# Corrected guesses for the row sums of the first attention, and down products interleaved with gate and up in the first feed forward

## The reference, cut to what matters

```
def _L0_xattn_ref(q, k, v, gamma):          # 8 heads over D = 256, 32 rows each
    qk = jnp.einsum('bhdq,bhdl->bhql', qh, kh) * scale
    sm = jax.nn.softmax(qk, axis=-1)
    ret = jnp.einsum('bhql,bhdl->bhdq', sm, vh)
    return gamma * ret.reshape(B, Dv, Lq)

def _L0_ffn_ref(x, gate_up_packed, gate_up_scales, down_packed, down_scales):
    w_gu = _dequant_fp4(gate_up_packed, gate_up_scales, 128)    # 2816 x 512
    w_down = _dequant_fp4(down_packed, down_scales, 128)        # 512 x 1408
    gate, up = split(jnp.einsum('bsh,oh->bso', x, w_gu))
    y = jnp.einsum('bsi,hi->bsh', jax.nn.silu(gate) * up, w_down)
    return y / jnp.sqrt(jnp.mean(y * y, axis=-1, keepdims=True) + 1e-6)

x = x + _L0_xattn_ref(_layernorm(x), ctx_2048, ctx_2048, gamma)
x = x + _L0_ffn_ref(_layernorm(x), ...)
x = x + _L1_xattn_ref(_layernorm(x), ctx_2048, ...)
x = x + _L1_ffn_ref(_layernorm(x), ...)
```

## Time and profile before

| | us |
|---|---|
| median of three runs | 2041.46 |
| profiled execution | 2041.32 |
| its span | 2039.7 |
| PE busy | 1789.8 (88% of the span) |
| DVE busy | 1562.4 (77%) |
| ACT busy | 1234.9 (61%) |
| POOL busy | 886.1 (43%) |
| dn_scale, 1408 KB, from issue at 402.8 to landing | 13.6 |
| raw_dn, 2816 KB, from issue at 402.3 to landing | 10.7 |

### The profile page before, as it was taken

How to read it: one execution, slowest core, us unless ns; L and a number is a source line. 1 busy time by engine, 2 the same in 40 slices (tenths; PEclk the granted TensorE clock), 3 DMA queues, 4 the chain that set the end, 5 groups by cost and what they waited for, 6 DMA issues and landing times. The chain is left out here.

```text
span 2039.7 us, 32890 instructions
## 1 busy us (share of the span) xinstructions
PE 1789.8 (88%) x11326; PEld 795.2 (39%) x11326; DVE 1562.4 (77%) x2892; ACT 1234.9 (61%) x2016; POOL 886.1 (43%) x908
## 2 busy tenths in 40 slices
PE   3997897688999987984989999999999988579998
PEld 0322222233344433542534444444444444234443
DVE  5899998582836627876899999999999965784433
ACT  4886776361644612441469999999999983322111
POOL 5565565160623510002038888888887880000000
PEclk9999999898999998996989999999999998789999
DMA  9764560010000002100025565555555544000000
GB/s 197 203 156 93 128 146 19 28 59 0 1 0 0 0 0 83 36 15 26 0 52 108 106 109 107 109 105 110 110 108 106 110 99 191 6 1 21 21 21 21
DMA packets 318045, 143.31 MB, mean 70 GB/s; under 512 B 273872, under 2 KB 290256, under 8 KB 316752
## 3 DMA queue, kind: packets, MB, share of 16 engines
q1 hardware_dynamic: 317904, 141.50, 31.1%
HBM read 70.15 MB, written 4.19 MB: 36 GB/s over the span
## 5 line engine op out<-in xcount | busy, mean ns | idle before, releaser
L1471 ACT ACTIVATE a_prob<-a_psS,a_bias,q_scale 128x1024 uint8<-128x1024 f32 x512 | 610.8, 1209 | 25.5 <-PE a_psS L1364 24.0
L1400 DVE TENSOR_REDUCE a_tops<-a_psM 128x1 f32<-128x512 f32 x1024 | 622.4, 675 | 1.8 <-PE a_psM L1354 0.3
L1450 POOL CAST a_wide<-a_pairs 128x2048 int16<-128x2048 uint8 x256 | 481.8, 1894 | 95.8 <-DMA a_pairs<-a_prob 87.5
L1354 PE MATMUL a_psM<-KT,QO 128*128 128x512 bf16 x1024 | 372.3, 387 | 5.9 <-PEq L1148 2.2
L1364 PE MATMUL a_psS<-KT,QO 128*128 128x512 bf16 x1024 | 305.2, 380 | 3.0 <-ACT a_prob L1471 3.0
L1376 PEld LDWEIGHTS a_psO<-V,a_wide 128*128 128x128 f16 x4096 | 175.2, 96 | 144.1 <-DVE QO L1413 23.0
L761 POOL TENSOR_TENSOR g_sum<-g_sum 128x512 f32<-128x512 f32 x88 | 126.8, 1441 | 197.6 <-DVE g_sum L826 197.6
L458 ACT ACTIVATE prob<-psT 128x512 f32<-128x512 f32 x256 | 145.5, 613 | 101.6 <-PE psT L637 101.0
L1376 PE MATMUL a_psO<-V,a_wide 128*128 128x32 bf16 x4096 | 181.3, 177 | 20.4 <-DVE QO L1413 15.6
L935 PE MATMUL g_psY<-raw_dn,g_hT 128*128 128x512 f32 x352 | 162.4, 622 | 26.3 <-DVE raw_dn L786 15.8
L514 DVE TENSOR_REDUCE rmax<-psS 128x1 f32<-128x512 f32 x256 | 161.4, 668 | 25.2 <-PE psS L623 25.2
(11 more groups left out here) (203 smaller groups left out, 2881.4 us busy)
## 6 DMA issues: line engine op xcount, KB each, us to landing
xs<-in_x SPq DMA_DIRECT2D x64, 256.0 KB, 7.9
cs<-in_ctx SPq DMA_DIRECT2D x64, 256.0 KB, 9.6
KT<-in_w SPq DMA_DIRECT2D x2, 4096.0 KB, 21.8
raw_gu<-in_gu SPq DMA_DIRECT2D x4, 1408.0 KB, 8.1
vs<-in_ctxT SPq DMA_DIRECT2D x16, 256.0 KB, 3.2
k_cT<-in_ctxT SPq DMA_DIRECT2D x16, 256.0 KB, 2.8
a_pairs<-a_prob SPq DMA_TRANSPOSE x256, 2.7
out<-x_sb SPq DMA_DIRECT2D x16, 256.0 KB, 2.0
```

What stands on the lines that cost most here:

```text
L1354: pe.matmul(psM[n % NM][:, :], QOf[:, i * P:(i + 1) * P], KTf[:, keys:keys + 512], start=True, stop=True).then_inc(shown, 1)
L1400: v.reduce_max(tops[i // JOIN % NB][:, i % JOIN, c:c + 1], psM[n % NM][:, :], AX.X).then_inc(topped, 1)
L1450: pool.tensor_copy(wide[i % NV][:, :, :, :].rearrange("p k c q -> p k (c q)"), both).then_inc(widened, 1)
L1471: act.activation(prob[i % NP][:, k * HK:(k + 1) * HK], psS[g % NS][:, :], ACT.Exp, scale=q_scale[:, i:i + 1], bias=bias[i // JOIN % NB][:, ...
```

## The change

In `mix_rows` the four reciprocals are gone. ACT now takes the logarithm of the sums and then the exponential of its negative (`logs`, `rinv`, both 128 x 512), which gives a guess of 1/s; DVE corrects the guess r to r (2 - s r) with two instructions at places 8 and 10, the second of them multiplied into `weighed`. The four parts of `collect` stand at the places 0, 1, 2 and 4.

The rows of the feed forward's first chunk are prepared inside `mix_rows`: in the last step DVE normalises them (`first_rows`), ACT makes the high part at places 10 to 13, POOL the low part, and SP transposes both with a DMA each. The normaliser of all 16 tiles moves into the feed forward, behind group 1 of chunk 0.

In `gated_ffn` the down products of group m - 3 stand between the two sides of group m and behind the second. At the fourth group of a chunk none stand, and two groups' worth at the fifth. The four tiles of rows have a bank `psY` each. The down weights come in three DMAs and are unpacked one group after the other: DVE moves and masks the bits, ACT gives the value, POOL multiplies with the scale. Later chunks are normalised, split and transposed by DMAs at groups 5 to 8 of the chunk before, so PE has no transposes left. The loop over the middle chunks is written out. Some semaphores are shared between blocks.

```
-    INVERT, STATS = (5, 7, 9, 11), (1, 3)
+    COLLECT, INVERT, STATS = (0, 1, 2, 4), (8, 10), (1, 3)
...
+                if i == 1:
+                    act.activation(e_sums[b][:, :], psE[:, :], ACT.Copy).then_inc(o_read, 1)
+                if i == 2:
+                    if j:
+                        act.wait_ge(rinv_ready, j)
+                    act.activation(logs[:, :], psE[:, :], ACT.Ln).then_inc(o_read, 1)
+                if i == 3:
+                    act.wait_ge(o_read, 3 * (j + 1))
+                    act.activation(rinv[b][:, :], logs[:, :], ACT.Exp, scale=-1.0).then_inc(rinv_ready, 1)
...
-                v.reciprocal(rinv[:, at], e_sums[j % 2][:, at]).then_inc(inverted, 1)
+                if i == 0:
+                    v.wait_ge(rinv_ready, j + 1)
+                    v.scalar_tensor_tensor(out=e_sums[b][:, :], in0=e_sums[b][:, :], scalar=-1.0, in1=rinv[b][:, :],
+                                           op0=ALU.mult, op1=ALU.mult).then_inc(corrected, 1)
+                if i == 1:
+                    v.wait_ge(corrected, j + 1)
+                    v.scalar_tensor_tensor(out=weighed[b][:, :], in0=e_sums[b][:, :], scalar=2.0,
+                                           in1=weighed[b][:, :], op0=ALU.add, op1=ALU.mult).then_inc(inverted, 1)
...
+            def first_rows():
+                own = Counter(v, env["norm_own"])
+                v.wait_ge(scales_in, 16)
+                own.count(v.tensor_copy(env["gu_scale"][:, :, :], gu_half[:, :, :]))
...
+                for k in range(TPC):
+                    v.tensor_scalar(xn[:, k, :], x_sb[:, k, :], env["mv"][:, k, 0:1], rstd[:, k:k + 1],
+                                    ALU.subtract, ALU.mult).then_inc(first_xn, 1)
...
+            def take_y(t, k):
+                v.wait_ge(squared, TPC * t + k + 1)
...
+                v.tensor_copy(y[t % 2][:, k, :], psY[k][:, :]).then_inc(y_taken, 1)
...
+                    for i in SIDES:
+                        fold(m, i)
+                        if t and p == TAKE:
+                            take_y(t - 1, 2 * i)
+                            take_y(t - 1, 2 * i + 1)
+                    if m:
+                        hidden(m - 1)
+                    if t == 0:
+                        unpack_down(p)
+                        if p == 1:
+                            normaliser(v, env)
+                    if t and p == ROOTS:
+                        finish_roots(t - 1)
...
+            def due(m):
+                groups = [m - LAG] if m >= LAG else []
+                if m % FG == LAG:
+                    groups = []
+                if m % FG == LAG + 1:
+                    groups = [m - LAG - 1, m - LAG]
+                return [(g // FG, g % FG, k) for g in groups for k in range(TPC)]
...
+                for p in range(FG):
+                    products = due(FG * t + p)
+                    half = len(products) // 2
+                    gate_up(t, p, 0)
+                    for t_f_k in products[:half]:
+                        down(*t_f_k)
+                    gate_up(t, p, 1)
+                    for t_f_k in products[half:]:
+                        down(*t_f_k)
```

457 lines of the change are left out of this document (259 added, 198 removed).

## The result

| | before | changed |
|---|---|---|
| median of the runs shown together | 2040.53 us (2029.74 to 2042.05) | 2004.23 us (2000.71 to 2005.01) |
| profiled execution: time, span | 2041.3, 2039.7 | 2004.9, 2003.1 |
| mixing, first row of maxima to last sum product | 346.5 | 349.2 |
| passage, last sum product to first gate product | 20.3 | 8.7 |
| feed forward, first gate to last down product | 353.2 | 324.2 |

The changed kernel is faster by 1.8%: ratio 0.9822, interval 0.9801 to 0.9843, well clear of no change. 2000 was forecast and the range was 1981 to 2018. The mixing starts 1.3 us earlier; 2.7 - 11.6 - 29.0 + 2.8 - 1.3 = -36.4 us, which is the difference of the two profiled executions.

A forecast was written before the change was run, and what follows sets the result against it. PE was taken to bound mixing steps without unpacking, DVE those with it, and product time plus stalls the feed forward. Mixing -3.0, passage -10.5 and feed forward -28.0 gave -41.5 from 2041.3: 2000 us, range 1981 to 2018.

The forecast's parts named there:

- The rival of a late transpose: Passage: a DMA transpose of the first chunk lands late and PE waits 6 us; 2006 us, chance 0.06.
- Between 16-bit and fp32 products ... 7.2: Feed forward: each of 80 changes between gate and down products costs PE 0.09 us, 7.2 us in all.
- The third rival: Feed forward: each change between gate and down costs 0.3 us, or a wait that size; +17, 2017 us, chance 0.12.
- At the fourth group ... 3.9: Feed forward, fourth group of chunks 1 to 3: ACT and DVE delay PE through psG, about 1.3 us each.
- Groups 0 to 3 of chunk 0 ... 25.8: Feed forward, groups without down products: 17.5 as before, 4.0 for DVE's bits, 4.3 for the normaliser; 25.8 us.
- The fourth rival: Feed forward: interleaved groups bound by psG, each of 80 half groups waits 0.65 us; +45, 2045 us, chance 0.04.
- +0.9 us a step, six steps: Mixing, steps without unpacking: ACT's logarithm and exponential stop PE by 0.48 and 0.43 us; +5.4 us in all.
- -1.05, eight times: Mixing, steps with unpacking: -1.05 behind the unpacking, +1.3 in front, -1.3 at the split; eight times, -8.4 us.
- I add 0.5 for POOL: Mixing, in front of the unpacking: 0.5 us a step for DVE waiting on POOL, on top of +0.8.
- The split's "-1.3": Mixing, steps with unpacking: DVE reaches the split 1 us earlier, half its collisions with POOL go; -1.3 us a step.
- The first rival: Mixing: DVE's relief comes through fully, every unpacking step gains 2.75 us, -22 instead of -3; 1981 us, chance 0.12.
- The second rival: Mixing: POOL holds both corrections a whole 1.15 us instruction in every unpacking step; +14, 2014 us, chance 0.10.

The follow-up runs named there:

- the second correction behind: Corrections at places 6 and 11 instead of 8 and 10, normaliser at group 4 instead of 1, against the changed kernel: 1999.02 us, ratio 0.9797 to the kernel before.

## Why the prediction was right, and where it was not

The time, the range and the sign came out, with 36.4 us gained where 41.5 were worked out. Of the three terms one was right in its parts, one came out right by errors that cancelled, and one failed:

**Passage: -10.5 forecast, -11.6 + 0.7 measured.** The trace agrees with the parts. Up to the end of DVE's last statistics it is 0.8 us shorter (0.6 forecast), and behind them 0.7 us are left of 11.5: -10.8 (10.9 forecast, as 4.3 and 6.6). The runs bear out the first part: with the reciprocals back the passage is 0.8 longer, without the corrections 1.5 shorter (1.6 forecast). The second was not undone in a run. The last step of the mixing, from its row of maxima to the last sum product, takes 17.6 instead of 16.8 us; that is the +1.0 for ACT's copies. The rival of a late transpose is out, since PE waits for the border alone.

**Feed forward: -28.0 forecast, -29.0 measured.** That the sum is right within 1 us is luck: three of its terms were wrong and cancelled.
- "Between 16-bit and fp32 products ... 7.2" was nothing. A full group takes 6.89 = 3.45 + 3.43 us. The 0.31 us of the earlier trace rows stands ahead of fp32 products of another shape (128*32), and I took it for the change of kind. The third rival is out.
- "At the fourth group ... 3.9": PE's four products there wait 0.5 us, not 1.3 (3.95 against 3.45), 1.5 in all.
- "Groups 0 to 3 of chunk 0 ... 25.8" was 30.5, and groups 6 to 9 took 7.42 instead of 6.89 (+2.1). The normaliser was counted at 4.3 and the bits at 4.0, each as DVE's own time. What was left out is that ACT waits for DVE in the order of its list (34.7 us in all), and PE for ACT; the run with the value later shows it for groups 0, 1 and 3, the one with the normaliser later for group 2. So -7.2 and -2.4 against +4.7 and +2.1: 323.1 of the 324.2 measured. The rest is 0.3 us in each of the fifth groups of chunks 1 to 3 (10.63 instead of 10.34) and 0.4 in the first group of chunk 1.

The fourth rival, the one on the slower side, could decide only where PE has no cover. It did not in the changed kernel; the run with bunched down products shows what it looks like.

**Mixing: -3.0 forecast, +1.9 measured for its 15 steps.** This is the step that failed, and in two places.
- Steps without unpacking, "+0.9 us a step, six steps": the mechanism was exact (0.94), the count was not. Of seven, four are of 18.69 us and become 19.63; the other three were already 19.7 to 20.3 us long for another reason (the one from 218.27 us a granted clock of 0.92; of the others it is open) and become 0.3 to 0.7 shorter. The sum over the seven is +2.3, not +5.4.
- Steps with unpacking, "-1.05, eight times": -0.3 over all eight instead of -8.4. "I add 0.5 for POOL" was too small: in seven of the eight steps the first correction waits 1.0 us for the last key (+3.1 against the forecast), and the second, which 0.67 was counted for, meets a query in three of them with 1.56 (+2.6). The split's "-1.3" was -0.9: the splits of the eight steps (the sum of their four instructions) fell from 20.0 to 12.8 us, not to 9.6 (+3.2). Not foreseen was that a start 1.3 us later changes what the unpacking meets: both casts blocked in four steps (4.73 us for its six instructions, 3.83 before), none in three (2.81), together +0.5. That is 9.4 against the 8.1 that are missing. The clock stands across these sums and had no term: four of the eight steps of the kernel before ran at a granted clock of 1.00 and three of the changed kernel's, and PE is busy 3.3 us longer over the eight (162.8 against 159.5 us). How the 8.1 divide between it and the waits of DVE is not shown.

The first rival, DVE's relief in full, is out: the mixing lost time, and without the corrections the steps without unpacking keep their 19.63 us.

The Trainium skill (SBUF — State Buffer, Who interferes with whom) says that a DVE instruction with two SBUF inputs contends with a GpSimd instruction that reads SBUF, and that one with at most one SBUF input outside the two-port modes does not. This case's traces agree with both halves: the correction takes 1.68 us beside POOL's keys and 0.67 alone, and the old reciprocals took 0.89 to 0.95 us beside POOL and alone. The prediction weighed the first half at 0.5 us a step, half a POOL instruction; the correction stood for 1.0. The second rival had this mechanism and priced it at 14 us over both corrections; it came to 3.1 + 2.6 = 5.7, since the second correction meets a query in three steps only.

With the first correction at place 6 the eight steps together are 9.3 us shorter than before, near the 8.4 us of the prediction. That is in part luck: in that kernel the second correction still takes 1.56 us in six of the eight steps and the split 2.47 in seven, both more than the prediction counted, and no step runs below a granted clock of 1.00, for which it had no term.

The best kernel of this study that still corrects the guess is the one with the first correction early, 1994.17 us (1994.53 with the normaliser later; the 1975.78 are for the guess alone): below both kernels, the second by an interval (0.9742 to 0.9784) that does not touch the changed kernel's.

What stays open: why the splits of some steps of the changed kernel are free and others not (0.72 to 2.47 us in the eight), which belongs to the same meeting of two lists but was not tried by itself; and when a wait of PE is followed by products at the lower level of the clock: with the second correction behind, seven steps have a wait of 2.9 to 3.0 us at the split, and three of them were. A place for the second correction that meets neither the queries nor the split was not found.

## What to carry to other kernels

Before an instruction with two SBUF inputs, a cast, or a TENSOR_SCALAR from SBUF to SBUF is moved on DVE, read from the timelines what POOL does at that time and at the time to which everything behind it is pushed: a small dependent chain (here the four instructions of the split) that runs into the other engine's work can cost more than the work that was moved. Compare steps at the same granted clock, since a wait of PE can be paid a second time in the products behind it. An instruction moved into a gap of its engine can still cost the engine next to it (here POOL's keys, 5.24 us instead of 4.65), and a term is best counted over the steps it applies to, not over all that look alike. Spreading one kind of product over a loop pays by the cover it gives the other engines, not by PE's time, so undo it in a test before the saving is credited to anything else.

## What the runs showed of the hardware

- DVE and POOL hold each other for most of an instruction, in both directions: a 128x512 correction 0.67 against 1.68 us, a 128x704 cast 0.52 against 1.47, a 128x512 integer mask 0.43 against 1.37, a 128x16 subtraction 0.17 against 1.01 to 1.18; POOL's subtractions 1.16 against 1.24 to 2.12. Maxima read from PSUM (`rmax<-psS`) keep 0.68 us beside POOL's work, and reciprocals of 128x128 from SBUF 0.94.
- A logarithm of 128 x 512 from PSUM and an exponential of it on ACT take 0.63 us and move the next one on by 0.48 and 0.52, like the softmax's exponentials (0.48 where two stand side by side).
- Going from 16-bit products to fp32 ones and back costs PE nothing: 0.22 us after a 16-bit product, 0.429 for each of the eight fp32 ones.
- Two steps with the same instructions and the same waits for POOL took 24.37 us at a granted clock of 1.00 and 25.86 at 0.93. Seven waits of PE of 2.03 us in the kernel with the first correction early were followed by products at the upper level, three of seven of 2.9 to 3.0 us in the kernel with the second correction behind by products at the lower.
